# A chunked scan with one y bank in place of two, five fill banks, clip and z read from PSUM, and a new job order

## What is computed

```python
xr, gate = split(x @ W_in.T)                 # 1024 channels each
xc = silu(conv4(xr + t_emb) + b_conv)        # causal, depthwise, 4 taps
xn = layernorm(xc) * ln_g + ln_b
B, C, dt = split(xn @ W_xproj.T)             # 16 states each
Ad = 1 - tanh(A_log) * tanh(dt @ W_dt.T + b_dt) * 0.01
Bd = B * minimum(norm(xn), 1)
h  = clip(h * Ad + Bd x xn, -10, 10)         # per token, h is 16 x 1024
y  = einsum(C, h) + D * xn
out = x + (y * silu(gate)) @ W_out.T
```

## Time and profile before

| | us |
|---|---|
| median of 3 runs | 2166.88 (2164.70 to 2167.35) |
| the profiled execution | 2165.86 |
| its span on the core | 2164.1 |
| TensorE busy in the span | 1949.7 (90%) |
| GpSimd busy | 1769.2 (82%) |
| VectorE busy | 1774.6 (82%) |
| ScalarE busy | 1434.0 (66%) |
| DMA engines, mean share | under 20% |

### The profile page before, as it was taken

One profiled execution on the slowest core, in us unless ns is written; L12 is line 12 of the kernel. 1 busy time (PEld: TensorE's weight loads), 2 busy tenths in 40 slices (PEclk: granted clock), 3 DMA queues, 4 the chain that ended last, 5 costly groups with the idle time before them and its releaser, 6 DMA issues.

```text
span 2164.1 us, 46979 instructions
## 1 busy us (share of the span) xinstructions
PE 1949.7 (90%) x16850; PEld 1432.7 (66%) x16850; DVE 1774.6 (82%) x2144; ACT 1434.0 (66%) x3462; POOL 1769.2 (82%) x1412
## 2 busy tenths in 40 slices
PE   5789999999999999999999999999999999999987
PEld 5466666666666666666666666666666666666654
DVE  3488888888888888888888888888888888888896
ACT  4677766767766767766767766767766767766743
POOL 1398888888888888888888888888888888888886
PEclk8699999999999999999999999999999999999999
DMA  5122121112121112121112121112121112121110
GB/s 169 54 57 58 45 59 43 56 56 58 44 59 43 56 55 59 44 59 43 55 56 58 44 59 43 56 56 59 44 59 43 56 55 59 44 59 43 51 50 15
DMA packets 81992, 118.07 MB, mean 55 GB/s; under 512 B 21840, under 2 KB 50896, under 8 KB 77088
## 3 DMA queue, kind: packets, MB, share of 16 engines
q1 hardware_dynamic: 81760, 115.07, 18.6%
HBM read 59.96 MB, written 9.18 MB: 32 GB/s over the span
## 4 chain that ended last, share of the span: by engine, by line
PE 47%; issue 19%; DVE 13%; ACT 11%; POOL 9%; DVEq 0%; DMA 0%; POOLq 0%; SPq 0%; ACTq 0%
PE ps_job L450 8%; PE ps_y L571 7%; POOL prod L1076 7%; PE ps_job L455 7%; PE ps_fill L554 6%; PE ps_fill L545 4%; ACT low L765 4%; DVE h L927 4%; DVE ks L980 3%; PE ps_y L561 3%; PE ps_job L496 2%; PE ps_job L462 2%; PE ps_job L477 2%; ACT tap L725 2%; PE ps_job L486 2%
## 5 line engine op out<-in xcount | busy, mean ns | idle before, releaser
L1076 POOL TENSOR_TENSOR prod<-ks,crep 128x512 f32<-128x512 f32 x1024 | 1301.0, 1283 | 290.4 <-PE ps_y L571 249.9
L980 DVE TENSOR_TENSOR_SCAN ks<-low,ps_fill 128x512 f32<-128x512 f32 x1024 | 1222.5, 1207 | 218.1 <-PE ps_fill L554 213.3
L765 ACT COPY low<-ps_fill 128x512 f32<-128x512 f32 x1024 | 593.3, 579 | 578.4 <-PE ps_fill L545 569.1
L571 PE MATMUL ps_y<-c_sb,prod 128*128 128x128 f32 x4096 | 621.2, 274 | 0.7 <-POOL prod L1076 0.6
L571 PEld LDWEIGHTS ps_y<-c_sb,prod 128*128 128x128 f32 x4096 | 463.4, 141 | 95.5 <-issue 33.9
L554 PE MATMUL ps_fill<-spans,pick 128*128 128x512 f16 x1024 | 392.4, 383 | 97.3 <-ACT low L765 95.1
L545 PEld LDWEIGHTS ps_fill<-ts,xs 128*128 128x128 f16 x4096 | 314.2, 98 | 145.5 <-issue 3.3
L545 PE MATMUL ps_fill<-ts,xs 128*128 128x128 f16 x4096 | 396.9, 219 | 1.0 <-DMA xs<-h 1.0
L725 ACT ACTIVATE tap<-xr,cols_sb 128x128 f32<-128x128 f32 x768 | 251.7, 392 | 0.1
L450 PE MATMUL ps_job<-x,w_in 128*128 128x128 f16 x3072 | 215.3, 221 | 27.5 <-issue 19.8
L554 PEld LDWEIGHTS ps_fill<-spans,pick 128*128 128x128 f16 x1024 | 99.3, 97 | 203.2 <-ACT low L765 164.4
(11 more groups left out here) (126 smaller groups left out, 2254.1 us busy)
## 6 DMA issues: line engine op xcount, KB each, us to landing
crep<-c_dram SPq DMA_DIRECT2D x32, 1024.0 KB, 4.8
xs<-xh SPq DMA_DIRECT2D x256, 64.0 KB, 2.0
xs<-xl SPq DMA_DIRECT2D x224, 64.0 KB, 2.0
xf<-in_xT SPq DMA_DIRECT2D x32, 256.0 KB, 2.9
res<-in_x SPq DMA_DIRECT2D x32, 256.0 KB, 2.7
out_dram<-res SPq DMA_DIRECT2D x32, 256.0 KB, 2.1
ts<-tth SPq DMA_DIRECT2D x128, 32.0 KB
ts<-tth SPq DMA_DIRECT2D x128, 31.0 KB
```

Of the source, the lines that this page charges most:

```text
L571: last = mm(ps_y[:, u // 4, cut], prod[:, s % HOLD, e, :], ident, start=False, stop=(u % 4 == 3 and q == 3 and e == QN - 1), is_transpose= ...
L765: copy(low[:, s % RING], ps_fill[:, s % RING]).then_inc(sem["low_copied"], 1)
L980: nc.vector.tensor_tensor_scan(ks[:, u % 2, QN * q:QN * (q + 1)].rearrange("d n t -> d (n t)"), low[:, s % RING], ps_fill[:, s % RING], 0. ...
L1076: tt(prod[:, i % HOLD], ks[:, u % 2, part], crep[:, p, part], ALU.mult).then_inc(sem["weighed"], 1)
```

## The change

One bank is taken from y and given to the fills: RING goes from 4 to 5 and AHEAD from 2 to 3, and `ps_y` has one bank, which both halves use in turn. `skip` for half 1 stands right behind `gated` of half 0 (GATED_AT[0], point 39), and `skip` for half 0 right behind `gated` of half 1 of the chunk before (point 7). At each turn TensorE leaves the flip of the half's first tile out of its slot and does two flips, behind `base`, in the next. The clip of h1 is now part of the take of `h0`: the sum is written back into the PSUM bank and a second instruction, a point later, reads it there, clips and writes `h1`, for each half; the instruction at point 28 is gone. Likewise z's first step is written back to PSUM and its second reads it there, both at point 5. The buffers for the taps go from 4 to 3. The jobs, the takes and the taps stand at new points; some waits are on other semaphores for that reason.

The diff, cut to its core ("..." marks what is left out):

```diff
-RING = 4
-AHEAD = 2
+RING = 5
+AHEAD = 3
 LAG = 4
 HOLD = 4
-TAPRING = 4
+TAPRING = 3
...
-        ps_y = S.enter_context(nc.psum_tensor("ps_y", [P, 2, BANK], F))
+        ps_y = S.enter_context(nc.psum_tensor("ps_y", [P, BANK], F))
...
-        JOBS = [(1, 3, "z", 0, 1, 1, 1), (1, 4, "gate", 0, 0, 2, 0), (5, 1, "hend", 0, -1, 2, 1),
-                (6, 4, "gate", 1, 0, 2, 0), (7, 1, "hend", 1, -1, 2, 1), (10, 1, "yT", 1, -1, 2, 1),
-                (15, 1, "zT", 0, 1, 1, 1), (17, 4, "xr", 0, 2, 2, 0), (20, 1, "h0", 0, 1, 2, 1),
-                (22, 4, "xr", 1, 2, 2, 0), (23, 1, "h0", 1, 1, 2, 1), (26, 1, "nb", 0, 1, 1, 1),
-                (28, 12, "conv", 0, 2, 2, 0), (30, 1, "carry", 0, 1, 2, 1), (34, 1, "carry", 1, 1, 2, 1),
-                (38, 14, "out", 0, -1, 1, 1), (44, 10, "conv", 1, 2, 2, 0), (54, 1, "yT", 0, 0, 2, 1),
+        JOBS = [(3, 2, "z", 0, 1, 1, 1), (3, 4, "gate", 0, 0, 2, 0), (6, 1, "hend", 0, -1, 2, 1),
+                (8, 4, "gate", 1, 0, 2, 0), (8, 1, "hend", 1, -1, 2, 1), (10, 1, "yT", 1, -1, 2, 1),
+                (15, 1, "zT", 0, 1, 1, 1), (19, 4, "xr", 0, 2, 2, 0), (21, 1, "h0", 0, 1, 2, 1),
+                (24, 4, "xr", 1, 2, 2, 0), (24, 1, "h0", 1, 1, 2, 1), (27, 1, "nb", 0, 1, 1, 1),
+                (33, 11, "conv", 0, 2, 2, 0), (32, 1, "carry", 0, 1, 2, 1), (36, 1, "carry", 1, 1, 2, 1),
+                (40, 13, "out", 0, -1, 1, 1), (46, 9, "conv", 1, 2, 2, 0), (54, 1, "yT", 0, 0, 2, 1),
                 (57, 1, "xt", 0, 2, 2, 0), (60, 1, "xt", 1, 2, 2, 0)]
...
-        TAKE = {("z", 0): 4, ("gate", 0): 5, ("hend", 0): 5, ("hend", 1): 7, ("yT", 1): 10, ("gate", 1): 11,
-                ("zT", 0): 15, ("h0", 0): 20, ("h0", 1): 23, ("xr", 0): 20, ("nb", 0): 26,
-                ("xr", 1): 25, ("carry", 0): 30, ("carry", 1): 34, ("conv", 0): 42, ("out", 0): 52,
-                ("conv", 1): 54, ("yT", 0): 54, ("xt", 0): 58, ("xt", 1): 62}
-        TAP_AT = [22, 28, 32, 36, 38, 40, 44, 46]
+        TAKE = {("z", 0): 5, ("gate", 0): 7, ("hend", 0): 6, ("hend", 1): 8, ("yT", 1): 10, ("gate", 1): 12,
+                ("zT", 0): 15, ("h0", 0): 21, ("h0", 1): 24, ("xr", 0): 23, ("nb", 0): 27,
+                ("xr", 1): 28, ("carry", 0): 32, ("carry", 1): 36, ("conv", 0): 44, ("out", 0): 53,
+                ("conv", 1): 55, ("yT", 0): 54, ("xt", 0): 58, ("xt", 1): 62}
+        TAP_AT = [24, 26, 32, 36, 39, 42, 45, 49]
...
-        GATED_AT = (42, 8)
+        GATED_AT = (39, 7)
...
                     t = s - LAG
-                    if t >= 0 and exists(k, 0):
-                        flip(k, p, t)
-                    elif t < 0 and exists(k, -1):
-                        flip(k - 1, 1 - p, t + TILES)
+                    if t % (4 * NQ) == 0:
+                        tiles = []
+                    elif t % (4 * NQ) == 1:
+                        tiles = [t - 1, t]
+                    else:
+                        tiles = [t]
+                    for t in tiles:
+                        if t >= 0 and exists(k, 0):
+                            flip(k, p, t)
+                        elif t < 0 and exists(k, -1):
+                            flip(k - 1, 1 - p, t + TILES)
...
+                    stt(bank("z")[:, 0:3 * NS], sums[:, 0, :], tiny[:, 2:3], bank("z")[:, 0:3 * NS], ALU.mult, ALU.add
+                        ).then_inc(sem["z0"], 1)
...
-                    stt(z[:], sums[:, 0, :], tiny[:, 2:3], bank("z")[:, 0:3 * NS], ALU.mult, ALU.add
+                    dve.wait_ge(sem["z0"], j + 1)
+                    stt(z[:], bank("z")[:, 0:3 * NS], tiny[:, 1:2], sums[:, 1, :], ALU.mult, ALU.add
                         ).then_inc(sem["z_taken"], 1)
-                if point == 6 and exists(k, 1):
-                    dve.wait_ge(sem["z_taken"], j + 1)
-                    stt(z[:], z[:], tiny[:, 1:2], sums[:, 1, :], ALU.mult, ALU.add).then_inc(sem["z1"], 1)
...
+                    stt(bank("h0", i)[0:NS], h1[:, half], first_decay[:], bank("h0", i)[0:NS], ALU.mult, ALU.add
+                        ).then_inc(sem["h0_sum"], 1)
+                for i in range(2):
+                    if point != TAKE["h0", i] + 1 or not exists(k, 1):
+                        continue
...
-                        stt(h1[:, half], h1[:, half], first_decay[:], bank("h0", i)[0:NS], ALU.mult, ALU.add
-                            ).then_inc(sem["h0_taken"], 1)
+                        dve.wait_ge(sem["h0_sum"], 2 * (j - BATCH) + i + 1)
+                    tsc(h1[:, half], bank("h0", i)[0:NS], CLIP, -CLIP, ALU.min, ALU.max
+                        ).then_inc(sem["h0_taken"], 1)
...
-                if point == 28 and exists(k, 1):
-                    dve.wait_ge(sem["h0_taken"], 2 * (j + 1))
-                    tsc(h1[:], h1[:], CLIP, -CLIP, ALU.min, ALU.max).then_inc(sem["h1_done"], 1)
...
-                since(dve, "y_gated", 2 * (k - 1) + i + 1)
+                since(dve, "y_gated", 2 * k + i)
...
                         if point == GATED_AT[0] and exists(k, 0):
                             gated(k, p, 0)
+                            skip(k, p, 1)
                         if point == GATED_AT[1] and exists(k, -1):
                             gated(k - 1, 1 - p, 1)
+                        if point == GATED_AT[1] and exists(k, 0):
+                            skip(k, p, 0)
                         side(k, p, point)
-                        if point == 43 and exists(k, 1):
-                            skip(k + 1, 1 - p, 0)
-                        if point == 9 and exists(k, 0):
-                            skip(k, p, 1)
...
-                    if s == 4 and exists(k, 1):
+                    if s == 3 and exists(k, 1):
                         pool.wait_ge(sem["squares"], j + 1)
```

More of the change, by code:

```diff
@@ L418, in _ @@
                 last.then_inc(sem["sums_ready"], 1)
-            for i in range(2):
-                last = mm(ps_y[:, i], pick[:], spans[:, 0, 0:BANK], start=True, stop=True)
-            last.then_inc(sem["y_opened"], 1)
+            mm(ps_y[:], pick[:], spans[:, 0, 0:BANK], start=True, stop=True).then_inc(sem["y_opened"], 1)
             pe.wait_ge(sem["sums_taken"], 1)
@@ L553, in widen @@
                 pe.wait_ge(sem["low_copied"], TILES * k + s + 1)
-                mm(ps_fill[:, s % RING], pick[:], spans[:, p, q * BANK:(q + 1) * BANK], start=False, stop=True,
+                mm(ps_fill[:, (TILES * k + s) % RING], pick[:], spans[:, p, q * BANK:(q + 1) * BANK], start=False, stop=True,
                    skip_group_check=True).then_inc(sem["bounded"], 1)
@@ L560, in base @@
                 pe.wait_ge(sem["skip_set"], 2 * k + i + 1)
-                mm(ps_y[:, i], mT[:, p], xn[:, p, half], start=False, stop=False, skip_group_check=True)
+                mm(ps_y[:], mT[:, p], xn[:, p, half], start=False, stop=False, skip_group_check=True)
             def flip(k, p, s):
@@ L570, in flip @@
                 for e in range(QN):
-                    last = mm(ps_y[:, u // 4, cut], prod[:, s % HOLD, e, :], ident, start=False,
+                    last = mm(ps_y[:, cut], prod[:, s % HOLD, e, :], ident, start=False,
                               stop=(u % 4 == 3 and q == 3 and e == QN - 1), is_transpose=True,
@@ L672, in side @@
                     copy(zm[0:1, 0], z[0:1, 0:2 * NS]).then_inc(sem["zm_high"], 1)
-                if point == 12 and exists(k, 2):
+                if point == 13 and exists(k, 2):
                     act.wait_ge(sem["xT_in"], 16 * (k + 3))
@@ L697, in side @@
                     copy(p_end[:, 1 - p:2 - p], pf[:, 1, P - 1:P]).then_inc(sem["p_kept"], 1)
-                if point == 24 and exists(k, 1):
+                if point == 21 and exists(k, 1):
                     act.wait_ge(sem["recip"], k + 2)
@@ L706, in side @@
                 if point == 41 and exists(k, 1):
[L707 removed]
+                    act.wait_ge(sem["h0_taken"], 2 * (k + 2))
                     if exists(k, 0):
@@ L743, in side @@
                     copy(lend[:, 1 - p, half], bank("carry", i)[0:NS]).then_inc(sem["lend_set"], 1)
-                if point == 27 and exists(k, 1):
+                if point == 28 and exists(k, 1):
                     act.wait_ge(sem["nb16"], 2 * (k + 2))
@@ L764, in copy_low @@
                     act.wait_ge(sem["filled"], TILES * k + s + 1)
-                    copy(low[:, s % RING], ps_fill[:, s % RING]).then_inc(sem["low_copied"], 1)
+                    copy(low[:, (TILES * k + s) % RING], ps_fill[:, (TILES * k + s) % RING]).then_inc(sem["low_copied"], 1)
                 for s in range(TILES):
@@ L840, in side @@
                 j, q = k + 1, (p + 1) % 2
-                if point == 46 and exists(k, 2):
+                if point == 48 and exists(k, 2):
                     dve.wait_ge(sem["conv_taken"], 2 * (k + 2) + 1)
@@ L844, in side @@
                     nc.vector.bn_stats(st[:, 0], xc[:, 0:BANK]).then_inc(sem["stats"], 1)
-                if point == 56 and exists(k, 2):
+                if point == 57 and exists(k, 2):
                     j2 = k + 2
```

(23 more changed lines are left out.)

10 lines of the change are left out of this document (5 added, 5 removed).

## The result

The changed kernel takes 2149.34 us (median of 4 runs, 2148.21 to 2151.48) against 2165.84 for the kernel before (also 4 runs): a recorded ratio of 0.9928, 95% interval 0.9913 to 0.9943. The quotient of the two medians, 0.9924, lies in that interval. It is faster by 16.5 us; I had forecast 36. The time lies in the range of 2080 to 2185, the sign is right, and the gain is less than half of the forecast. The profiled execution spans 2149.7 us, 14.4 less than before.

What follows compares the result with a forecast made beforehand. TensorE's fixed order, with 7.7 us of stops in each 64.9 us step, was taken to bound the kernel. Gains less 3.3 of costs, net 1.2 a step over 31 steps, gave 37 us off: 2130 us, range 2080 to 2185.

Steps and rivals of the forecast that it cites:

- the take of carry half 1 behind ScalarE's taps: Tap sets at points 32 and 36 delay carry's takes; TensorE stops 1.0 us a step at carry half 1.
- base and yT half 1 behind VectorE's queue at the turn: With one y bank, TensorE stops 0.9 us a step at base half 1 and 1.3 at yT half 1.
- a copy stop behind xn: At widen, ScalarE's copy behind xn comes about 0.85 us late, to which the ring adds 0.15.
- one at carry half 0: Round slots 12 to 16, the stop moves from widen to carry half 0, which needs ScalarE's bqm: 0.7 us.
- out's 0.4: At out, in carry's bank, the taps delaying carry's take were to cost a stop of 0.5 us a step.
- Net 1.2: Whole step: gains less 3.3 us of costs shorten it by 1.2 us, from 64.9 to 63.7.
- 0.3 of small stops: TensorE's small stops in each step: 0.3 us counted among the gains.
- Start and end have the same work: nothing: Before and after the steps: the same work, so no change in time.
- 31 equal steps: Whole span: the 1.2 us gained in each of 31 steps takes 37 us off.
- The cover: Rival: ScalarE and VectorE run ahead, a third of 4.3 us new stops is absent; 2086 us, chance 0.20.
- GpSimd, held at the turns: Rival: products wait for flips at two turns a step; step 65.0 to 66.0 us, up to 2201, chance 0.26.
- The clip out of PSUM: Forecast 0.68 us per half on VectorE; the rival said 1.3, 0.9 a step worse, 2158 us, chance 0.05.

Runs made afterwards that it cites:

- e3: The changed kernel with ScalarE taking carry ahead of the taps at points 32 and 36: 2113.72 us, ratio 0.9762.
- e4: The changed kernel with gate half 0 taken at point 6, ahead of ScalarE's square of xn, in place of 7: 2149.88 us, ratio 0.9925.
- e5: The changed kernel with yT half 1, its job and takes, one point later at 11: 2124.77 us, ratio 0.9811.
- e6: The changed kernel with the D term left out but for 32 of 512 columns of each half, so skip is short: 2117.62 us, ratio 0.9777.
- e10: The kernel of e9 with xt half 1 in the other job bank: 2075.20 us, ratio 0.9579 to the kernel before.
- e11: The changed kernel with z and gate half 0 back at their old points: 2182.33 us, ratio 1.0072 to the kernel before.
- e2: The changed kernel with clip and z's second step done as before, not out of PSUM: 2151.14 us, ratio 0.9939.
- e1: The kernel before with only the clip and z's second step reading PSUM: 2159.57 us, ratio 0.9972.
- e9: The changed kernel with the moves of e3, e4 and e5 together: 2072.02 us, ratio 0.9569 to the kernel before.

## Why the prediction was wrong in size

**The mechanism was right in the main.** The stops that carry most of the forecast are there, behind the engine that was named: the take of carry half 1 behind ScalarE's taps (shown by e3), base and yT half 1 behind VectorE's queue at the turn (e4, e5, e6), a copy stop behind xn, one at carry half 0 (the 0.53 at 1093.41, by its place the one for ScalarE's bqm). Three differ. out's 0.4 was forecast as 0.5 for the taps; e3 shows that it is not theirs, so this term came near by luck. gate half 1 (0.51) is not in the forecast; e4 shows that it is one stop with yT half 1, and the two together (1.45) are near the 1.3 put down for yT. xt half 1 (0.54), which waits for ScalarE's take of half 0, is not in it either; with the 0.35 of widen behind xn it makes 0.9, where 1.0 was put down for widen, and e10 shows that the one turns into the other. GpSimd stands 2.55 at the turn of half 1 and 1.87 at that of half 0, where I had 3 and under 1, and gives it back. Its timeline:

```profile
1073.65 3.73 POOL L1085 TENSOR_TENSOR prod<-ks,crep 128x512 f32<-128x512 f32 x3 [1.87 <-PE ps_y L569]
...
1104.93 2.50 POOL L1085 TENSOR_TENSOR prod<-ks,crep 128x512 f32<-128x512 f32 x2 [2.55 <-PE ps_y L569]
```

**The step that failed is the sum.** Net 1.2 was to be the difference of 4.5 gained and 3.3 paid, and what was measured is 0.65. Too small were carry half 1 (1.0, measured 1.25), the turn of half 0 (1.3, measured 1.45), what is left of the stops behind ScalarE's queue (1.7, measured 1.85) and xr half 1 (nothing, measured 0.3); too large were h0 and the gain of 0.3 from small stops. In detail: xr half 1 waits for ScalarE's take of half 0, in the same bank, which now comes with the taps at points 24 and 26 round it. h0 stops 0.25 less than forecast, zT and out 0.1 less each; why h0 does is not shown. Together the terms of the table are 0.45 worse than forecast (6.75 against 6.3). The other term is the "0.3 of small stops", which I counted as gained without naming what would end them. What the step holds beside the 57.2 of work and the stops of the table was 64.9 - 57.2 - 7.3 = 0.4 and is 64.25 - 57.2 - 6.75 = 0.3, so most of them are still there. None of the terms is off by more than 0.3; together they are half of the net.

**Start and end have the same work: nothing.** Wrong by some 4 us at the start, and by 2.3 the other way at the end. The first step is 68.5 us, where it was 65.7, since z and gate stand behind the fill that waits for VectorE, which still splits the weights (e11). The second is 1.1 above the later ones, and there, too, skip took 2.8 us.

**31 equal steps.** In the profiled execution one more step, the nineteenth, takes 67.05 us; the section on the hardware tells of it. From the spans: 30 steps at 0.65 less are 19.5 off; the first step, the second and the nineteenth put back 2.8, 1.1 and 2.8, other steps 0.6, and the end takes off 2.3. That is 14.5 by the rounded terms, and the spans differ by 14.4.

**The clip isn't what carry waits for.** I had written that its gain is used up by the taps; e2 shows that the clip is worth nothing in the new order. The stop of the earlier trace rows was the clip's, as I had read it: in e1 it is gone. But the step is only 0.2 shorter for it, not 1.0, since other waits, z's among them, take the time up.

**Rivals.** The cover is not what happened: the stops of carry and the turns are as long as forecast or longer. Nor did GpSimd, held at the turns, decide: TensorE does not wait for products, and e9 with 2.6 us less a step shows how far that was from deciding. The clip out of PSUM is cheap, 0.67 for each half.

## What to carry to other kernels

In an order written by hand the stops that stand ahead of one late instruction are one stop: taking away the first (e4, e10) gives its time to the next, and what shortened the step here was to take work out of the queue ahead of the take that is waited for (e3, e6), or to put the waiting job behind other work (e5). So before a net of many terms is trusted, ask for each gain what the engine waits for next, and give a net that is the small difference of large sums the error of all of its terms. Where two engines' side work is listed at the same point, look up which of them stands first: here two takes, each behind 1.3 us of taps nobody waited for, cost 36 us of 2149 (e3), more than twice what the change had gained.

## What the runs showed of the hardware

A VectorE instruction with two inputs in SBUF seems able to wait for more than one of GpSimd's. skip takes 0.70 us at the turn of half 1, where GpSimd stands, and 1.64 to 1.67 at that of half 0, where it began inside a product (1.56 in the earlier trace rows). The Trainium skill (SBUF — State Buffer, Who interferes with whom) says that the second to issue is blocked until the first is through; the usual 1.64 agrees, and so does e6, where skip on 32 columns took 0.20 and 1.14: the same wait of about 0.95 at either size. But in the nineteenth step it took 2.94 us, beside four products in a row on GpSimd. Timelines of the two engines in the changed kernel:

```profile
1260.81 2.94 DVE L978 TENSOR_TENSOR ps_y<-xn,row_d 128x512 f32<-128x512 f32 x1
```

```profile
1258.16 4.99 POOL L1085 TENSOR_TENSOR prod<-ks,crep 128x512 f32<-128x512 f32 x4
1263.08 1.06 POOL L1045 TENSOR_TENSOR tiny<-tiny,halfs 128x1 f32<-128x1 f32 x1
```

The four products start 1.24 apart, so one ended near 1261.9 and the next near 1263.1; skip ended at 1263.75, as if it had been passed over at the first of these. That it was passed over is inferred; that it took 1.3 us more than its neighbours is measured. A skip of 2.7 to 2.9 stands in nine of the fourteen profiles, one to three times among the 64, and never in that of the kernel before, whose longest was 1.56.

What followed was not expected either. TensorE stood 2.00 us at yT half 1 in place of 0.72, and then the granted clock was at its lower level, 1.2 GHz, for some 3.3 us (0.52 in the row by windows): eight flips in 1.88 where eight at full clock take 1.04.

```profile
1265.59 0.66 PE L488 MATMUL ps_job<-c_sb,gate 128*128 128x128 f32 x4 [2.00 <-DVE h L885]
1266.05 1.91 PE L559 MATMUL ps_y<-xn,mT 128*128 128x512 f32 x2
1267.75 1.88 PE L569 MATMUL ps_y<-c_sb,prod 128*128 128x128 f32 x8
```

The same eight flips three steps earlier, at full clock:

```profile
1072.90 1.04 PE L569 MATMUL ps_y<-c_sb,prod 128*128 128x128 f32 x8
```

The granted clock, from the view by windows:

```profile
1265.90:1269.20 3.30, 3.30 (x12) 2.16 (x11) 1.36 (x2) 0.70 (x2) 0.24 (x1) 0.52 0.31 70
```

The columns of this row are: length, busy time of TensorE, its weight loads, VectorE, ScalarE and GpSimd, the granted clock, the DMA share and GB/s. The step was 2.8 us longer: the wait is 1.3 more, and from the start of base to the end of the flips it took 1269.46 - 1266.05 = 3.41 us, where it took 1.73 three steps earlier at full clock (1072.04 to 1073.77). That the stop brought the clock down is not shown. In the second step of the same profile TensorE stood even longer at the same job, behind a skip of 2.80, and the granted clock stayed at 1.00; that step is 1.2 longer than the later ones.

```profile
171.69 0.63 PE L488 MATMUL ps_job<-c_sb,gate 128*128 128x128 f32 x4 [2.22 <-DVE h L885]
```
